# Time mixing on one core: VectorE's row mix moved ahead of the key spans, blocks moved on TensorE, and a loop of 28 turns instead of 4

## The reference

```python
xx = xprev - x
xxx = x + xx * time_maa_x
mix = tanh(xxx @ maa_w1.T)                       # 128 hidden, in four groups f
xrg, xwa, xk, xv = x + xx * (time_maa + einsum(mix, maa_w2))
r = xrg @ receptance.T;  g = tanh(xrg @ gate_w1.T) @ gate_w2.T
k = xk @ key_w.T;  v = xv @ value.T              # plus low-rank terms for kk, w, a, ma, mk
# 16 heads of 32 channels, token by token:
S = S * exp(w) + (S @ kk) b^T + v k^T;  y = S @ r
out = ((group_norm(y) + bonus(r, k) * v) * g) @ output.T
```

## Time and profile before

| | |
|---|---|
| median of 3 runs | 6792.22 us (6789.73 to 6812.12) |
| profiled execution | 6799.37 us, its span 6797.6 us |
| mean granted TensorE clock over the span | 0.949 |
| TensorE, matmuls | 6026.9 us (89%) |
| TensorE, weight loads | 4343.0 us (64%) |
| VectorE | 4002.5 us (59%) |
| ScalarE | 1878.1 us (28%) |
| GpSimd | 1458.2 us (21%) |

### The profile page before, as it was taken

The page is one execution under the profiler, slowest core; times in us unless marked ns, Lnnn a source line. Parts: engine busy times, 40 slices in busy tenths (PEclk is TensorE's granted clock), DMA queues, the critical chain, the costliest instruction groups (busy, mean ns, idle before and its releaser), DMA issues. The chain is left out here.

```text
span 6797.6 us, 270041 instructions
## 1 busy us (share of the span) xinstructions
PE 6026.9 (89%) x123464; PEld 4343.0 (64%) x123464; DVE 4002.5 (59%) x9325; ACT 1878.1 (28%) x3531; POOL 1458.2 (21%) x1284
## 2 busy tenths in 40 slices
PE   6888888888889888888888888888489999999999
PEld 5777777777777777777777777777334444444444
DVE  5777777777777777777777777777442223222310
ACT  3333333333333333333333333333100000000000
POOL 1222122222212222221222222222021122112220
PEclk8999999999999999999999999999689999999999
DMA  1000000000000000000000000000212211221120
GB/s 54 16 20 16 16 22 16 16 18 20 16 16 22 16 16 18 20 16 17 21 16 16 18 20 16 17 21 11 69 44 70 77 55 62 71 67 65 56 76 13
DMA packets 108728, 212.84 MB, mean 31 GB/s; under 512 B 25424, under 2 KB 26704, under 8 KB 107088
## 3 DMA queue, kind: packets, MB, share of 16 engines
q1 hardware_dynamic: 92240, 144.98, 7.4%
q0 software_dynamic: 15360, 50.48, 2.2%
HBM read 144.67 MB, written 50.72 MB: 29 GB/s over the span
## 5 line engine op out<-in xcount | busy, mean ns | idle before, releaser
L377 DVE COPY_PREDICATED time_raw<-time_known,w_bank 128x96 f32<-128x96 int32 (+6 forms) x3072 | 826.0, 273 | 226.5 <-PE w_bank L877 146.8
L1662 PE MATMUL moe_bank<-moe_w,moe_hidden 128*128 128x512 f32 x2048 | 928.7, 596 | 0.0
L1649 PE MATMUL moe_bank<-moe_hT,moe_w 128*128 128x512 f32 x2048 | 923.2, 594 | 0.8 <-DVE moe_hT L1549 0.8
L1649 PEld LDWEIGHTS moe_bank<-moe_hT,moe_w 128*128 128x128 f32 x2048 | 386.3, 190 | 471.2 <-issue 470.1
L1662 PEld LDWEIGHTS moe_bank<-moe_w,moe_hidden 128*128 128x128 f32 x2048 | 379.4, 190 | 429.5 <-issue 428.1
L1570 ACT ACTIVATE moe_hidden<-moe_bank,moe_b 128x512 f32<-128x512 f32 x256 | 175.9, 687 | 1628.2 <-PE moe_bank L1649 1523.1
L806 POOL TENSOR_TENSOR time_tail<-time_tail,time_lp 128x512 f32<-128x512 f32 x64 | 75.4, 1178 | 2414.1 <-ACT time_lp L733 2350.3
L864 PE MATMUL w_bank<-time_invT,time_part 32*32 32x32 f32 x32768 | 437.1, 204 | 71.5 <-issue 50.2
L402 DVE COPY_PREDICATED time_invT<-time_levels,w_bank 128x512 f32<-128x512 int32 x256 | 187.1, 731 | 499.7 <-PE w_bank L864 499.7
L864 PEld LDWEIGHTS w_bank<-time_invT,time_part 32*32 32x32 f32 x32768 | 373.0, 116 | 152.9 <-issue 98.3
L853 PE MATMUL w_bank<-time_inv,time_ub 32*32 32x32 f32 x32768 | 401.5, 196 | 77.6 <-ACT time_yT L617 30.6
(11 more groups left out here) (227 smaller groups left out, 10038.5 us busy)
## 6 DMA issues: line engine op xcount, KB each, us to landing
moe_w<-in_w SPq DMA_DIRECT2D x64, 1024.0 KB, 7.3
mid_xn<-time_xn_rows SPq DMA_DIRECT2D x128, 129.0 KB, 2.5
time_x_rows<-in_x SPq DMA_DIRECT2D x128, 128.0 KB, 2.8
time_base<-in_x SPq DMA_DIRECT2D x128, 128.0 KB, 3.3
mid_acc<-time_mixed SPq DMA_DIRECT2D x128, 128.0 KB, 2.7
mid_scores<-time_rated SPq DMA_DIRECT2D x128, 2.0 KB, 2.2
...
```

Of the source, the lines that this page charges most:

```text
L377: e.copy_predicated(by_raw[:, "uy".index(q), n0:n1, :, 0:8 * j + 8], known[:, "uy".index(q), :, :, mine].to_broadcast([P, n1 - n0, 2, 8 * ...
L1649: got = e.matmul(up[now % 3][:, :], w1[:, g * F + k * P:g * F + (k + 1) * P], hT[x % 2][:, g * CAP + half * HALF:g * CAP + (half + 1) * HA ...
L1662: got = e.matmul(down[t][:, :], hidden[now % 4][:, t * P:(t + 1) * P], tile(w2, k), start=k == 0, stop=k == FC - 1)
```

## The change

It does four things. On VectorE, xx and xxx stand first in a turn; row mix 1 (lerp1, xf1) stands ahead of `make_keys(2)`; the transposition uk (L413) and the masks of u0 come behind the second inversion and row mix 2. On ScalarE, the exponential of spans 0 to 2 stands behind the tanh. On TensorE, the second value block joins the first ahead of P0, u2 moves behind two key blocks, u3 behind the last key block, y5 ahead of y4. The loop holds 28 turns and runs twice. The step lists are changed alike; one line of each form stands at the head of the diff. No operation is added or removed.

```diff
@@ PE_STEPS
-            "B.u1 B.u2 A.low_k C.P2 B.u3 C.Q2 A.key A.decay C.P3 B.u4 B.u5 A.low2 C.Q3 B.y0 B.y1 A.sums C.z0 B.y2 "
+            "B.u1 A.low_k C.P2 B.u2 C.Q2 A.key B.u3 A.decay C.P3 B.u4 B.u5 A.low2 C.Q3 B.y0 B.y1 A.sums C.z0 B.y2 "
@@ on_vector
             enter(e, dve, "dve", turn)
+            if A:
+                e.wait_ge(act.sem, act["A.x"])
+                e.tensor_tensor(by_b(xx), xs[:, :, :, 0:TB], xnow, ALU.subtract).then_inc(dve.sem, dve.step("A.xx"))
...
             if Bs:
                 query_span()
                 key_span(3)
@@
                 e.bn_aggr(mv[:, :], stats[:, :]).then_inc(dve.sem, dve.step("N.mv"))
-            if A:
-                e.wait_ge(act.sem, act["A.x"])
-                e.tensor_tensor(by_b(xx), xs[:, :, :, 0:TB], xnow, ALU.subtract).then_inc(dve.sem, dve.step("A.xx"))
...
@@
+            if A:
+                lerp_of(1)
             if Bs:
                 make_keys(2)
-            if A:
-                lerp_of(1)
-            if Bs:
                 make_keys(1)
                 make_keys(0)
...
-            if Cs:
-                turn_scores([(1, "uk")])
             if D:
...
+            if Cs:
+                invert(1)
+            if A:
+                lerp_of(2)
+            if Cs:
+                turn_scores([(1, "uk")])
             if Bs:
                 mask_scores("u", 0)
-            if Cs:
-                invert(1)
-            if A:
-                lerp_of(2)
-            if Bs:
                 mask_scores("u", 1)
@@ on_scalar
                 e.activation(key_units(1, 3), key_units(1, 3), ACT.Exp).then_inc(act.sem, act.step("B.ek3"))
+            if Cs:
+                part_of(0)
+            if A:
+                e.wait_ge(pe.sem, pe["A.mix"])
+                e.activation(col(mix), BANK["mix"][:, 0:P], ACT.Tanh).then_inc(act.sem, act.step("A.mix"))
+            if Bs:
                 e.wait_ge(dve.sem, dve["B.dk0"])
...
-            if Cs:
-                part_of(0)
-            if A:
-                e.wait_ge(pe.sem, pe["A.mix"])
-                e.activation(col(mix), BANK["mix"][:, 0:P], ACT.Tanh).then_inc(act.sem, act.step("A.mix"))
@@ on_tensor
-                value_of(0, 1)
+                value_of(0, 2)
             if Cs:
                 P_of(0, 0)
-            if Bs:
-                value_of(1, 2)
@@
                 score("u", 1)
-                score("u", 2)
@@
                 key_of(0, 2)
+            if Bs:
+                score("u", 2)
             if Cs:
                 Q_of(2, 0)
+            if A:
+                key_of(2, 3)
+            if Cs:
+                Q_of(2, 1)
+            if A:
+                key_of(3, 4).then_inc(pe.sem, pe.step("A.key"))
             if Bs:
                 score("u", 3)
-            if Cs:
-                Q_of(2, 1)
-            if A:
-                key_of(2, 4).then_inc(pe.sem, pe.step("A.key"))
@@
             if Bs:
+                score("y", 5)
                 score("y", 4)
-                score("y", 5)
@@ the loop
+LONG = 28
-        with nc.Fori(0, tiles // SETS - 2) as four:
-            for i in range(SETS):
-                step(four * SETS + (i + 1), SETS + 1 + i, "NABCD")
+        turns = (tiles - 8) // LONG
+        with nc.Fori(0, turns) as part_of_tiles:
+            for i in range(LONG):
+                step(part_of_tiles * LONG + (i + 1), SETS + 1 + i, "NABCD")
```

More of the change, by code:

```diff
@@ L256, in time_mix @@
         ACT_STEPS = (
-            "A.carried A.x B.ek3 B.ek012 C.P0 A.mix D.squares B.eq D.lnv N.lnv D.rstd N.rstd B.v C.P1 A.hid_g A.hid_w A.hid_a "
+            "A.carried A.x B.ek3 C.P0 A.mix B.ek012 D.squares B.eq D.lnv N.lnv D.rstd N.rstd B.v C.P1 A.hid_g A.hid_w A.hid_a "
             "D.affine0 D.affine1 D.affine2 D.affine3 A.hid_kkk A.hid_mk C.P2 A.exp_z A.tail A.k C.P3 A.tna A.tnma "
@@ L263, in time_mix @@
             "A.x D.centre C.P0 A.mix A.scored C.Q0 D.var A.delta D.gate B.value C.P1 B.bonus A.gate1 A.low_wa A.delta3 B.u0 C.Q1 "
-            "B.u1 B.u2 A.low_k C.P2 B.u3 C.Q2 A.key A.decay C.P3 B.u4 B.u5 A.low2 C.Q3 B.y0 B.y1 A.sums C.z0 B.y2 "
-            "B.y3 C.u0 C.y0 D.out B.y4 B.y5 C.z1 C.u1 A.recept C.y1").split()
+            "B.u1 A.low_k C.P2 B.u2 C.Q2 A.key B.u3 A.decay C.P3 B.u4 B.u5 A.low2 C.Q3 B.y0 B.y1 A.sums C.z0 B.y2 "
+            "B.y3 C.u0 C.y0 D.out B.y5 B.y4 C.z1 C.u1 A.recept C.y1").split()
         BANK = Banks(psum, [
@@ L429, in on_vector @@
             enter(e, dve, "dve", turn)
+            if A:
+                e.wait_ge(act.sem, act["A.x"])
+                e.tensor_tensor(by_b(xx), xs[:, :, :, 0:TB], xnow, ALU.subtract).then_inc(dve.sem, dve.step("A.xx"))
+                e.wait_ge(dve.sem, dve["A.xx"])
+                for g in range(G):
+                    e.scalar_tensor_tensor(
+                        grp(xxx, g).rearrange("p (b t) -> p b t", b=B), grp(xx, g).rearrange("p (b t) -> p b t", b=B),
+                        wt["maa_x"][:, g:g + 1], xs[:, g, :, 1:TB + 1], ALU.mult, ALU.add).then_inc(
+                        dve.sem, dve.step(f"A.xxx{g}"))
             if Bs:
@@ L438, in on_vector @@
                 e.bn_aggr(mv[:, :], stats[:, :]).then_inc(dve.sem, dve.step("N.mv"))
-            if A:
-                e.wait_ge(act.sem, act["A.x"])
-                e.tensor_tensor(by_b(xx), xs[:, :, :, 0:TB], xnow, ALU.subtract).then_inc(dve.sem, dve.step("A.xx"))
-                e.wait_ge(dve.sem, dve["A.xx"])
-                for g in range(G):
-                    e.scalar_tensor_tensor(
-                        grp(xxx, g).rearrange("p (b t) -> p b t", b=B), grp(xx, g).rearrange("p (b t) -> p b t", b=B),
-                        wt["maa_x"][:, g:g + 1], xs[:, g, :, 1:TB + 1], ALU.mult, ALU.add).then_inc(
-                        dve.sem, dve.step(f"A.xxx{g}"))
             if Bs:
@@ L467, in on_vector @@
                 e.tensor_tensor(col(mixed), col(BANK["centre"]), col(rstd), ALU.mult).then_inc(dve.sem, dve.step("D.normed"))
-            if Bs:
-                make_keys(2)
             if A:
@@ L472, in on_vector @@
             if Bs:
+                make_keys(2)
                 make_keys(1)
@@ L493, in on_vector @@
                 lerp_of(2)
+            if Cs:
+                turn_scores([(1, "uk")])
             if Bs:
+                mask_scores("u", 0)
                 mask_scores("u", 1)
@@ L638, in on_scalar @@
                 e.activation(col(mix), BANK["mix"][:, 0:P], ACT.Tanh).then_inc(act.sem, act.step("A.mix"))
+            if Bs:
+                e.wait_ge(dve.sem, dve["B.dk0"])
+                e.activation(by_key[:, :, 1, 0:key_at(3)], by_key[:, :, 1, 0:key_at(3)], ACT.Exp).then_inc(
+                    act.sem, act.step("B.ek012"))
             if D:
@@ L1040, in on_tensor @@
                 key_of(0, 2)
+            if Bs:
+                score("u", 2)
             if Cs:
                 Q_of(2, 0)
-            if Bs:
-                score("u", 3)
+            if A:
+                key_of(2, 3)
             if Cs:
@@ L1047, in on_tensor @@
             if A:
-                key_of(2, 4).then_inc(pe.sem, pe.step("A.key"))
+                key_of(3, 4).then_inc(pe.sem, pe.step("A.key"))
+            if Bs:
+                score("u", 3)
             if Cs:
```

4 lines of the change are left out of this document (removed), and 8 rows, old and new, of the table DVE_STEPS.

## The result

The changed kernel takes 6585.38 us (median of 4 runs, 6582.06 to 6597.02) against 6790.98 us (4 runs) of the kernel before: ratio 0.9695, 95% interval 0.9675 to 0.9715. The forecast was 6670, range 6545 to 6785. The profiled execution has a span of 6580.5 us and a mean granted clock of 0.955 (before 0.949).

What follows compares the result with a forecast made beforehand. TensorE, idling at fixed waits, was the bound: pattern turn 71.04 − 2.1 − 0.45 = 68.5 us, with low clock (2.1) and gaps (1.5) 72.1 against 74.31; 2.2 × 60 turns = 132 us off 6799.4 gave 6670, range 6545 to 6785.

Steps and rivals of the forecast that it cites:

- Bound and pattern turn: TensorE bounds the kernel, idling at fixed places; a 71.04 us turn without "issue" gaps is the pattern, mean turn 74.31.
- Mix ahead of spans: VectorE's xx starts 2.57 us sooner; before the mixing matmuls 0.85 us of wait is left where 0.67 + 2.69 stood.
- Q0: TensorE's Q0 newly waits 0.5 us for ScalarE's copy of P0, which stands behind key span 3's exponential.
- Row mix 1 ahead of keys 2: On VectorE, xf1 is ready by about 1258.8, so TensorE's 1.26 us wait before L838 is gone.
- The held products and the wait at u0: GpSimd's query run holds VectorE's six key products to 5.5 us (low bound 4.1); u0 waits 3.0 us for the bonus.
- First masks and u blocks: P2 waits 0.6 us, low_k 1 us but starts 3.2 us sooner; u2 costs 1.1, third level starts 2.1 us sooner.
- y5 ahead of y4: On TensorE, y5 fills the 0.85 us wait for the output sum; 0.45 us of it counted per turn.
- Loop of 28: 12 branches fewer; bounds 0 and 43 us, taken as 0 because VectorE catches up during the idle time.
- branches were a real cost: Rival: nothing is won back after a branch, so 43 us more go, 6627; chance 0.10.
- The clock takes the gain: Rival: more low-clock stretches and fetch gaps take back 2.1 us per turn, about 6795, no change; chance 0.11.
- slower: Rival: late keys and bonus make u0 wait; from 5.5 us the kernel is slower, with 6.5 us 6880; chance 0.12.
- Not held: Rival: key products take 4.1 us, u0 waits 1.6, one low stretch or none; 6526, half of it 6600; chance 0.22.

Runs made afterwards that it cites:

- a1: The changed kernel with the loop of 4 turns as before instead of 28: 6632.9 us, ratio 0.9745.
- a4: The kernel before with only xx and the masked mixes first on VectorE: 6784.7 us, ratio 0.9984.
- c1: b4 with ScalarE copying P0 ahead of the exponential of span 3: 6411.6 us, ratio 0.9436.
- b4: The changed kernel, complete, with GpSimd's y query products made only after VectorE's last key product: 6438.8 us, ratio 0.9468.
- b1: The changed kernel with keys 2 ahead of row mix 1 again on VectorE: 6568.1 us, ratio 0.9662.
- b3: The changed kernel with GpSimd's y query products cut to one unit of sixteen, so computation is left out: 6388.7 us, ratio 0.9391.
- c2: c1 with GpSimd's rk product and identity copy waiting for VectorE's last product of keys 3: 6377.1 us, ratio 0.9398.
- d1: b4 with row mix 2 and xf2 ahead of the output gate's sum and product on VectorE: 6510.6 us, ratio 0.9584.
- b2: The changed kernel with uk, u0's masks, u2 and u3 back at their places of before: 6588.3 us, ratio 0.9684.
- a3: The changed kernel with score block y4 ahead of y5 again: 6614.5 us, ratio 0.9741.
- a2: The kernel before with only the loop changed, to 28 turns: 6797.1 us, ratio 0.9989.

## Why the prediction was right or wrong, point by point

- **Bound and pattern turn.** Right: waits at fixed places, and the clock behind the longest. The clean turn takes 69.91 us, which answers to my 68.5 + 2.1 = 70.6; the mean one 70.78 for 72.1. 1.3 × 60 = 79 of the 85 us between 6670 and 6585 lie here. Half of the 1.3 is in the clean turn, behind u0: the slow stretch cost less than I had priced (see the first masks, below). The other half is in what a mean turn takes beyond it: I had 1.5 us, and it is 0.9 (70.78 − 69.91). The 1.5 came from the turns of the old loop, in which the branches' idle time is 0.9 us a turn, and I had not taken it out; a1 puts 0.6 to 0.8 us a turn on the branches. Both misses lie on the same side, so the range held, but the gain was 206 us for 132.
- **Mix ahead of spans.** L975 waits 1.15 us in the clean turn and 0.7 in the mean of all turns for my 0.85; GpSimd's rk product held the state sum ahead of xx, before as now. That ScalarE's order decides was in the working ("the wide exponential ... would have made it longer"); a4 shows that without it nothing is gained at all.
- **Q0.** 0.45 us for 0.5; c1 shows that it was a true cost in b4's order, 22 us by the ratios and 27 by the medians.
- **Row mix 1 ahead of keys 2.** The 1.26 us wait is gone as said; b1 shows that this alone is worth nothing, since the wait returns at u0.
- **The held products and the wait at u0.** The step on which the forecast stood, and in the clean turn the chosen bound was right: 5.5 us for the six, against 5.55 measured, with three held and xf1 too, as I had it. Over all turns they take 4.9: the 256-wide product by b takes 1012 ns on average and the one by k 0.5 us, not 1.4 us as I gave for a sign, and the fourth wide product mostly came when GpSimd's were over. The low bound of 4.1 us was no bound: it was read off a turn in which products are held already, and b4 shows 2.4 for the six when none is. The Trainium skill, "SBUF — State Buffer", section "SBUF: two separate sides", has the rule of the shared port pair, locked for a whole instruction, and b3, b4, c2 and d1 agree: the same product takes 0.55 or 1.54 us. The wait at u0 was 2.3 us on average, not 3.0, but that shortened no turn: u0 starts 24.5 us into the turn, in the clean turn as in the mean, for my 24.3, and TensorE is only ready for it later, after 22.0 us for my 21.3. A wait can be shorter than forecast because the one who waits comes late.
- **First masks and u blocks.** Wrong in detail: I had 0.6 us at P2 and 1.0 before low_k; in the clean turn they were 0 and 0.5, in the mean 0.1 and 0.8. The slow stretch behind u0 lengthens u0, u1 and the halves of Q1 and P2 behind them by 2.4 us in sum, and VectorE catches up meanwhile, so it hides waits. I had priced two stretches at 2.0 us with a third hidden; that put the start of the third level 0.1 us sooner than before the change, and it is 0.8 us sooner (35.5 us into the turn for 36.3). The 0.7 us are 42 us of the error in 60 turns. In the turn of b4 shown, where these blocks run at full clock, the waits at u1, P2 and low_k are 0.84, 0.40 and 0.99 us. b2 shows the edit itself to be worth at most some 18 us, so the "2.1 us" in my sum were not the edit's but came from u0's earlier start.
- **y5 ahead of y4.** 0.45 us forecast, 31 us in 60 turns by a3 (0.52).
- **Loop of 28.** The term that was mis-sized. I took 0 because the old kernel gives the idle time back; a2 confirms this for the old order. But it was given back at L977, by the very wait that the first edit removes, and a1 shows 34 to 47 us: the price of the rival "branches were a real cost" (43), whose 6627 was nearer than my 6670. The rule of the Trainium skill, "Runtime: NRT & Kernel Launch", section "Instruction fetch mechanics", that unrolling is preferred is borne out in the new order only.
- **The clock.** I expected two low stretches of 3.4 us behind u0; the turn shown has 6.7 us at 1.2 GHz there, the mean turn 6.4 in all, and the mean clock stayed at 0.95 as implied. "The clock takes the gain" did not come, and "slower" neither: u0's wait never came near 5.5 us.
- **Not held.** It did not come in this kernel. b4, in which the six products are held by nothing, takes 6439; I had 6526 for it, with 4.1 us for the six where b4 has 2.4.

In sum, by parts: xx with the exponential −2.3%, loop −0.5%, y5 −0.5%, u blocks 0, row mix 1 +0.3%: −2.9% of the 3.05% measured. The second value block ahead of P0 has no run of its own; the rest would leave it 0.1 to 0.2%, less than these runs can tell.

c2 is faster than both kernels, 6377 us, with one more wait in each of two places of GpSimd and two lines of ScalarE exchanged.
